# A graph-network kernel: gated sums of two destination tiles accumulated in PSUM and added once, with half-tile weight buffers

## The chip, the cores and the metric

The kernel runs on one core of a Trainium2 chip. The time is that of the device, in microseconds (us), from the first to the last instruction with what the launch adds around them. The median of three runs counts.

## The reference

Four layers of a graph network over 6250 nodes with 128 features and 206250 edges, sorted by destination. Each layer normalises the rows, applies a relu, sums rows over edges, and adds to `x`. Only the first layer weights its edges, and it is the one that the change touches.

```python
h = jnp.maximum(_layernorm(x, axis=-1), 0.0)
g = sigmoid(h @ W_gate + b_gate)
m = g * (h @ W)
msgs = edge_weight[:, None] * m[dst]
x = x + segment_sum(msgs, src, num_segments=6250)   # first layer
x = x + segment_sum(h[src], dst) @ W1.T + b1        # second; third and fourth alike
```

## The kernel before

**Tiles and stages.** Nodes are cut into 49 tiles of 128 (`TILES`). Five stages follow one another: a preparation (to about 130 us in the profile), the *count stage* (to about 1328 us), and three and a bit more stages (`ph` 1 to 4) that multiply by count matrices read back from DRAM (`by_source`). The change lies in the preparation and the count stage.

**One step of the count stage** (`build(j, k, c)` on each engine) handles destination tile `j`, with 128 edge slots in 64 windows. DVE makes one-hot operands out of the edge records in eight groups of eight windows (`hots`: L882, L883, L885), in `HOT_SLOTS` = 3 buffers. PE multiplies them (`half_windows`, L602 to L604: 12 matmuls of 98 columns in each of 16 *units*), which gives the plain counts and the weighted counts of this destination against all 49 source tiles, in one of three pairs of PSUM banks. ACT copies plain counts and the high half of the weighted ones to `stage` (L1174, `hi_done`); PE subtracts the high half in PSUM (`take_high`, L585), and ACT copies the rest, the low half (L1159, `lo_done`). PE cannot be more than two units ahead of those copies: before unit `u` it subtracts the high half of unit `u-2`, which waits for its `hi_done`.

**The SP queue** (`hand_on`) then hands the tile on, in order: a small load `g_in`, a DMA that transposes the high weights (49 blocks of 128x128) into `wt`, the same two for the low weights, and a store of the plain counts to DRAM. `stage` and `wt` each have two buffers, by the parity of the tile. ACT waits at the first unit of tile `j` until the store of tile `j-2` has landed (`stored0`, `stored1`), and SP waits for `hi_done` of the whole tile.

**The gated sums.** `sum_four(t, b, g)` multiplies four blocks of `wt` of tile `t` with its gated rows `g_in`: 12 matmuls of 128 columns into one of two PSUM banks (L577 to L579), 147 in a tile. DVE adds each bank to `X` (`add_four`, L897), 13 times in a tile. PE does this for tile `j-2` while it builds tile `j`, two such fours behind each group of windows.

**The loop.** `tiles_loop` writes out 13 tiles and then loops three times over 12. All engines have the same shape. The edge records (`meta`, `meta_w`) of all 25 pairs of tiles stay in SBUF; the preparation fills them in five batches.

Of the kernel before, what the change touches and what calls it, by code (L numbers as in the profile page):

```python
# [19 lines left out]
P = 128  # L20
# [38 lines left out]
FULL = TILES + TILES % 2  # L59
SET_COLS = HALF * WD  # L60
# [27 lines left out]
def summed_at(h):  # L88

    return range(2 * h, min(2 * h + 2, FOURS))  # L90
# [64 lines left out]
def gnn_kernel(nc, x, src, dst, edge_weight, w0, wg0, bg0, w1, b1, wm, bm, wu, bu, hyper, w3, b3, gamma, beta, out):  # L155
    ctx = ExitStack()
    with ctx:
# [21 lines left out]
        table = nc.dram_tensor("edge_table", (ROWS, 3 * ALIGN), I32).ap()  # L179
        by_source = nc.dram_tensor("counts_by_source", (FULL // 2, P, TILES, 2, P), F16).ap()  # L180
# [16 lines left out]
        mv = keep("mv", [P, TILES, 2], F32)  # L197
# [13 lines left out]
        meta, o = at("meta", [P, GROUPS, 2, P // 2, 2], F16, base0)  # L211
        meta_w, o = at("meta_w", [P, WINDOWS // 2, WEIGHTS, 2], F16, o)
# [28 lines left out]
        G, o = at("G", [P, TILES, 2, P], F16, wt_at)  # L241
        pre, r = at("pre", [P, BATCH, 2, P], F16, o)
# [95 lines left out]
        def _(sp):  # L338
# [18 lines left out]

            def turn_keys(m):

                lot = batch(m)  # L360
                sp.wait_ge(s("pre"), m + 1)
                sp.dma_start_transpose(meta[:, lot.start:lot.stop].rearrange("e n a q b -> e (n a) (q b)"),
                                       pre[:].rearrange("q n a e -> q (n a e)")).then_inc(s("keys_in"), 16)
                if m:
                    sp.wait_ge(s("meta_w"), m)
# [9 lines left out]
            for m in range(3):  # L375
                turn_keys(m)
            store_gated(0)
# [4 lines left out]
            for c in range(3, SET):  # L382
                store_gated(c)

            def layers(general):
                if general:
                    for a, b in ((dst, dst_pad), (src, src_pad), (edge_weight.bitcast(I32), w_pad)):
                        sp.dma_start(b[0:EDGES].rearrange("(a b) -> a b", a=15), a.rearrange("(a b) -> a b", a=15)).then_inc(s("pad_in"), 16)
# [8 lines left out]
                sp.wait_ge(s("g_stored"), 16 * SET)  # L397

                def hand_on(j, k, c):

                    b = c % 2
                    if later(j, 2):
                        sp.wait_ge(s("four_done"), (j - 1) * FOURS)
                    for a, done in enumerate(("hi_done", "lo_done")):
                        part = slice(a * P, (a + 1) * P)
                        sp.wait_ge(s(done), (j + 1) * HALVES)
                        sp.dma_start(g_in[:, b, part], slab(g_dram, j)[:, part]).then_inc(s(f"g_loaded{b}"), 16)
# [289 lines left out]
        def _(dve):  # L697
# [172 lines left out]
            def layers(general):  # L870
# [59 lines left out]
                def split(ph):  # L930

                    if ph == 1:
                        counts_stored(dve)
# [360 lines left out]
```

## Time and profile before

| what | value |
|---|---|
| median of three runs | 2605.35 us (2597.77 to 2607.53) |
| the profiled execution | 2608.04 us |
| its span | 2606.2 us |
| busy PE / DVE / ACT | 2320.7 / 1603.8 / 1230.0 us |
| DVE adds of L897 | 637, 392.4 us busy |
| matmuls of L577 to L579 | 3 x 2401 |
| stores of counts, transposes into `wt` | 49 and 98 DMAs |

Busy time is what an engine spent inside instructions. A busy PE is not a PE at its peak, since its matmuls overlap. The granted clock is the share of full speed that TensorE got: 1.00 is 2.4 GHz and 0.50 is 1.2 GHz.

### The profile page before, as it was taken

The numbers are of one execution on the slowest core, as the hardware profiler recorded it, in microseconds if no ns is written. First come the engines' busy times: TensorE is split into PE (matmuls) and PEld (weight loads), VectorE is DVE, ScalarE is ACT, GpSimd is POOL, SyncE is SP. The second block draws the span as 40 slices with busy tenths as digits, with TensorE's granted clock in tenths as the row PEclk, the third lists the DMA queues.
The fourth block names the chain that finished last, engine by engine and source line by source line (L and its number), as shares of the span: only waits on it lengthen the run. The fifth ranks groups of instructions, "written<-read, shape, count | busy, mean of one in ns | idle before, by whom it ended". The sixth has DMA issues, their size and how long they took to land. (4 is left out here: it accounts for less than half of the span.)

```text
span 2606.2 us, 71305 instructions
## 1 busy us (share of the span) xinstructions
PE 2320.7 (89%) x27901; PEld 1993.0 (76%) x27901; DVE 1603.8 (62%) x3678; ACT 1230.0 (47%) x2680; POOL 44.6 (2%) x51
## 2 busy tenths in 40 slices
PE   2489999999989998999929999899998999999996
PEld 1368778878777887887828888788887888888884
DVE  6689999999999998999962333334433112121224
ACT  2478878878777786877731222222232000011113
POOL 3300000000000000000000000000000000000000
PEclk8589999999999998999969999999998999999996
DMA  6479999999999999999989999899998999999994
GB/s 191 106 157 201 216 214 208 210 218 209 212 181 220 212 212 175 222 199 212 218 211 251 283 285 283 223 260 258 258 259 208 290 288 290 263 246 248 266 270 110
DMA packets 1608879, 589.27 MB, mean 226 GB/s; under 512 B 964326, under 2 KB 1605354, under 8 KB 1608471
## 3 DMA queue, kind: packets, MB, share of 16 engines
q1 hardware_dynamic: 1604773, 579.88, 99.9%
q0 software_dynamic: 1600, 4.92, 0.7%
q8 instruction: 191, 3.13, 0.5%
q10 hardware_dynamic: 2226, 0.62, 0.2%
q14 instruction: 89, 0.73, 0.1%
HBM read 255.26 MB, written 89.20 MB: 132 GB/s over the span
## 5 line engine op out<-in xcount | busy, mean ns | idle before, releaser
L1174 ACT CAST stage<-ps 128x784 f16<-128x784 f32 x784 | 655.4, 836 | 106.0 <-DMA counts_by_source<-stage 69.7
L649 PE MATMUL ps<-Ha,a_tiles 128*128 128x258 f16 x4802 | 548.5, 274 | 46.6 <-ACT Ha L1221 39.2
L649 PEld LDWEIGHTS ps<-Ha,a_tiles 128*128 128x128 f16 x4802 | 470.1, 98 | 117.1 <-ACT Ha L1221 39.3
L602 PE MATMUL ps<-hot_c,hot_r 128*128 128x98 f16 x3136 | 509.5, 212 | 13.6 <-DVE hot_c L885 7.4
L603 PE MATMUL ps<-hot_c,hot_r 128*128 128x98 f16 x3136 | 503.5, 211 | 0.0
L604 PE MATMUL ps<-hot_c,hot_r 128*128 128x98 f16 x3136 | 501.7, 210 | 0.0
L1159 ACT CAST stage<-ps 128x392 f16<-128x392 f32 x784 | 397.9, 508 | 142.5 <-PE ps L585 142.5
L577 PE MATMUL ps<-g_in,wt 128*128 128x128 f16 x2401 | 431.0, 222 | 35.9 <-DVE X L897 17.3
L578 PE MATMUL ps<-g_in,wt 128*128 128x128 f16 x2401 | 429.3, 222 | 0.0
L579 PE MATMUL ps<-g_in,wt 128*128 128x128 f16 x2401 | 429.2, 222 | 0.0
L897 DVE SCALAR_TENSOR_TENSOR X<-ps,X 128x512 f32<-128x512 f32 (+1 forms) x637 | 392.4, 650 | 49.4 <-PE ps L579 49.3
L602 PEld LDWEIGHTS ps<-hot_c,hot_r 128*128 128x128 f16 x3136 | 308.7, 98 | 95.8 <-ACT stage L1159 53.0
L885 DVE TENSOR_TENSOR hot_c<-hot_c,meta_w 128x1568 f16<-128x1568 f16 x392 | 378.6, 966 | 0.0
L603 PEld LDWEIGHTS ps<-hot_c,hot_r 128*128 128x128 f16 x3136 | 310.5, 99 | 19.2 <-issue 1.9
L585 PE MATMUL ps<-stage,minus 128*128 128x392 f16 x784 | 262.9, 335 | 59.2 <-ACT stage L1174 30.8
L604 PEld LDWEIGHTS ps<-hot_c,hot_r 128*128 128x128 f16 x3136 | 309.9, 99 | 0.0
L649 PE MATMUL ps<-Hb,a_turned 128*128 128x258 f16 x2401 | 277.9, 274 | 14.3 <-DMA a_turned<-counts_by_source 12.0
L649 PE MATMUL ps<-Hb,a_tiles 128*128 128x258 f16 x2401 | 278.4, 274 | 7.2 <-ACT Hb L1200 7.2
L577 PEld LDWEIGHTS ps<-g_in,wt 128*128 128x128 f16 x2401 | 238.0, 99 | 59.7 <-DVE X L897 42.9
L649 PEld LDWEIGHTS ps<-Hb,a_turned 128*128 128x128 f16 x2401 | 233.4, 98 | 52.0 <-DMA a_turned<-counts_by_source 15.2
L649 PEld LDWEIGHTS ps<-Hb,a_tiles 128*128 128x128 f16 x2401 | 235.1, 98 | 48.1 <-ACT Hb L1200 7.4
L883 DVE TENSOR_TENSOR hot_r<-iota_r,meta 128x1024 f16<-128x1024 f16 x392 | 267.5, 682 | 0.0
(194 smaller groups left out, 2062.1 us busy)
## 6 DMA issues: line engine op xcount, KB each, us to landing
a_tiles<-counts_by_source SPq DMA_DIRECT2D x147, 1600.0 KB, 8.8
counts_by_source<-stage SPq DMA_DIRECT2D x49, 1600.0 KB, 8.0
gated_parts<-G SPq DMA_DIRECT2D x7, 448.0 KB, 3.6
g_in<-gated_parts SPq DMA_DIRECT2D x98, 32.0 KB, 3.1
out_x<-X SPq DMA_DIRECT2D x6, 512.0 KB
edge_table<-tab SPq DMA_DIRECT2D x1, 2448.0 KB, 10.5
wt<-stage SPq DMA_TRANSPOSE x98, 10.9
dst_run<-in_dst SPq DMA_DIRECT2D x1, 612.4 KB
```

Of the source, the lines that this page charges most:

```text
L577: mm(o, wt[:, b, 0, i], g_in[:, b, 0:P], start=i % 4 == 0, stop=False, skip_group_check=True)
L578: mm(o, wt[:, b, 0, i], g_in[:, b, P:2 * P], start=False, stop=False, skip_group_check=True)
L579: last = mm(o, wt[:, b, 1, i], g_in[:, b, 0:P], start=False, stop=True, skip_group_check=True)
L602: mm(into(0), rows_, codes(0), start=v == 0, stop=True, skip_group_check=True)
L603: mm(into(1), rows_, codes(1), start=v == 0, stop=False, skip_group_check=True)
L604: last = mm(into(1), rows_, codes(2), start=False, stop=True, skip_group_check=True)
L649: last = mm(ps[:, c % 2, 0:PARTS], a_slot(ph, c, i), moving[:, i], start=i == 0, stop=i == TILES - 1)
L883: v.tensor_tensor(hot_r[:, b], iota_r[:].unsqueeze(1).to_broadcast([P, PAIRS, P, 2]), key(0, P), ALU.is_equal)
L885: v.tensor_tensor(hot_c[:, b, :, 1:1 + WEIGHTS], hot_c[:, b, :, 0].unsqueeze(2).to_broadcast([P, PAIRS, WEIGHTS, WCOLS, 2]), meta_w[:, pai ...
L897: v.scalar_tensor_tensor(xs, ps[:, 6 + e, 0:(hi - lo) * P], 1.0 / (W_UP * H_UP), xs, ALU.mult, ALU.add).then_inc(s("added"), 1)
L1159: a.copy(stage[:, b, 2, 0:TILES, u * SET_COLS:(u + 1) * SET_COLS], of).then_inc(s("lo_done"), 1)
L1174: a.copy(stage[:, b, 0:2, 0:TILES, u * SET_COLS:(u + 1) * SET_COLS], of).then_inc(s("hi_done"), 1)
```

## The change

1. **Sums of two tiles in PSUM.** `sum_four` now works on a pair of tiles: for each of four source tiles it accumulates the three products of the first tile and the three of the second in the same bank, 24 matmuls, and `add_four` adds the bank once. The fours of a pair are spread over two steps: six (`FIRST`) in the odd tile behind groups 1 to 6, seven in the even tile after it, behind groups 0 to 6. They come one tile later than before: pair `n` (tiles `2n`, `2n+1`) is summed in tiles `2n+3` and `2n+4`.
2. **Half-tile weight buffers.** A tile's weights are held in two halves (24 and 25 blocks), in six homes that rotate (`HOMES`), so each transposing DMA becomes two. `stage` keeps its two buffers, one block each shorter.
3. **Edge records streamed.** The preparation turns the records into `keys_b` and `weights_b`, stores them by pair of tiles to DRAM (`edge_groups`), and SP loads the record of pair `p+2` (128 KB) when the one-hot operands of pair `p` are done. The interleaving copy on POOL becomes two copies.

```diff
+def fours_at(c, h):
+    if c % 2:
+        return range(h - 1, h) if 1 <= h <= FIRST else range(0)
+    return range(FIRST + h, FIRST + h + 1) if FIRST + h < FOURS else range(0)
...
-        stage, o = at("stage", [P, 2, 1 + WEIGHTS, FULL, P], F16, o)
+        stage, o = at("stage", [P, 2, PARTED, P], F16, o)
-        wt, o = at("wt", [P, 2, WEIGHTS, TILES, P], F16, o)
-        g_in, o = at("g_in", [P, 2, 2 * P], F16, o)
+        wt, o = at("wt", [P, 6, WEIGHTS, len(HALF_TILES[1]), P], F16, o)
+        g_in, o = at("g_in", [P, 4, 2 * P], F16, o)
...
+            def store_groups(m):
+                lot = batch(m)
+                sp.wait_ge(s("meta_w"), m + 1)
+                sp.wait_ge(s("keys_in"), 16 * (m + 1))
+                to = groups[lot.start:lot.stop].rearrange("n e x -> e n x")
+                sp.dma_start(to[:, :, 0:KEYS], keys_b[:, m % 2]).then_inc(s("meta_stored"), 16)
+                sp.dma_start(to[:, :, KEYS:], weights_b[:, m % 2]).then_inc(s("meta_stored"), 16)
...
                 def hand_on(j, k, c):
-                    b = c % 2
-                    if later(j, 2):
-                        sp.wait_ge(s("four_done"), (j - 1) * FOURS)
+                    b, pair = c % 2, pair_of(k, c)
+                    if b:
+                        sp.wait_ge(s("hot_ready"), j * TILE_HOTS + TILE_HOTS)
+                        sp.dma_start(meta[:, to], of).then_inc(s(f"meta_in{to}"), 16)
+                    if b and later(j, 2):
+                        sp.wait_ge(s("four_done"), (pair - 1) * FOURS + FIRST)
+                    elif later(j, 4):
+                        sp.wait_ge(s("four_done"), (pair - 1) * FOURS)
                     for a, done in enumerate(("hi_done", "lo_done")):
                         sp.wait_ge(s(done), (j + 1) * HALVES)
-                        sp.dma_start_transpose(wt[:, b, a], stage[:, b, 1 + a, 0:TILES].rearrange("p i d -> p (i d)")).then_inc(s(f"wt_in{b}"), 16)
+                        for half, tiles in enumerate(HALF_TILES):
+                            first = FULL + a * TILES + tiles.start
+                            sp.dma_start_transpose(wt[:, home(c, half), a, 0:len(tiles)],
+                                                   stage[:, b, first:first + len(tiles)].rearrange("p i d -> p (i d)")).then_inc(s(f"wt_in{b}"), 16)
...
-                def sum_four(t, b, g):
+                def sum_four(n, cp, g, both=True):
-                    n, e = t * FOURS + g, (b + g) % 2
+                    f, e = n * FOURS + g, (cp + g) % 2
                     for i in range(4 * g, min(4 * g + 4, TILES)):
                         o = ps[:, 6 + e, (i % 4) * P:(i % 4 + 1) * P]
-                        mm(o, wt[:, b, 0, i], g_in[:, b, 0:P], start=i % 4 == 0, stop=False, skip_group_check=True)
-                        mm(o, wt[:, b, 0, i], g_in[:, b, P:2 * P], start=False, stop=False, skip_group_check=True)
-                        last = mm(o, wt[:, b, 1, i], g_in[:, b, 0:P], start=False, stop=True, skip_group_check=True)
+                        for b in range(1 + both):
+                            at_ = wt[:, home(c, half), :, i - HALF_TILES[half].start]
+                            mm(o, at_[:, 0], g_in[:, c % 4, 0:P], start=i % 4 == 0 and b == 0, stop=False, skip_group_check=True)
+                            mm(o, at_[:, 0], g_in[:, c % 4, P:2 * P], start=False, stop=False, skip_group_check=True)
+                            last = mm(o, at_[:, 1], g_in[:, c % 4, 0:P], start=False, stop=True, skip_group_check=True)
                     last.then_inc(s("four_done"), 1)
```

**On DVE**, the rows from the last groups of an odd tile written out ahead of the loop to the first group of the next tile. Before, two adds stand behind a group, one short add at the end of a tile's fours, and one group has none (`meta` and `meta_w` hold the records):

```order
L897 SCALAR_TENSOR_TENSOR X<-ps,X 128x512 [waits added,four_done] x2
L882 TENSOR_TENSOR hot_c<-iota_c,meta 128x4x196 [waits unit_done]
L883 TENSOR_TENSOR hot_r<-iota_r,meta 128x1024
L885 TENSOR_TENSOR hot_c<-hot_c,meta_w 128x4x392 [waits hot_codes]
L897 SCALAR_TENSOR_TENSOR X<-ps,X 128x128 [waits added,four_done]
L882 TENSOR_TENSOR hot_c<-iota_c,meta 128x4x196 [waits unit_done]
L883 TENSOR_TENSOR hot_r<-iota_r,meta 128x1024
L885 TENSOR_TENSOR hot_c<-hot_c,meta_w 128x4x392 [waits hot_codes]
```

In the changed kernel, over the same kind of boundary (`meta` holds keys and weights of a pair):

```order
L962 SCALAR_TENSOR_TENSOR X<-ps,X 128x512 [waits added,four_done]
L947 TENSOR_TENSOR hot_c<-iota_c,meta 128x4x196 [waits meta_in0,unit_done]
L948 TENSOR_TENSOR hot_r<-iota_r,meta 128x1024
L950 TENSOR_TENSOR hot_c<-hot_c,meta 128x4x392 [waits hot_codes]
L962 SCALAR_TENSOR_TENSOR X<-ps,X 128x512 [waits added,four_done]
L947 TENSOR_TENSOR hot_c<-iota_c,meta 128x4x196 [waits unit_done]
L948 TENSOR_TENSOR hot_r<-iota_r,meta 128x1024
L950 TENSOR_TENSOR hot_c<-hot_c,meta 128x4x392 [waits hot_codes]
```

At most one add now stands behind a group, and the first group of a pair waits for its record.

**On the SP queue**, one tile in the loop before (an ISA row is a wait or an address):

```order
L406 ISA [waits four_done]
L407 ISA [waits hi_done]
L407 DMA g_in<-gated_parts 128x128
L408 DMA_TRANSPOSE wt<-stage 128x49x128
L407 ISA [waits lo_done]
L407 DMA g_in<-gated_parts 128x128
L408 DMA_TRANSPOSE wt<-stage 128x49x128
L409 ISA
L409 DMA counts_by_source<-stage 128x25x256
```

and one odd tile of the changed kernel:

```order
L446 ISA [waits hot_ready]
L446 DMA meta<-edge_groups 128x512
L449 ISA
L454 ISA [waits four_done]
L455 ISA [waits hi_done]
L455 DMA g_in<-gated_parts 128x128
L458 DMA_TRANSPOSE wt<-stage 128x24x128
L458 DMA_TRANSPOSE wt<-stage 128x25x128
L455 ISA [waits lo_done]
L455 DMA g_in<-gated_parts 128x128
L458 DMA_TRANSPOSE wt<-stage 128x24x128
L458 DMA_TRANSPOSE wt<-stage 128x25x128
```

The store of the counts (L460) follows as before. Two more DMAs stand between a tile's last copy and its store, and an odd tile's record load stands ahead of them.

## Rows read from the trace of the kernel before

**Rows 1.** Windows, 300:600: busy time by engine, clock, DMA share, GB/s

```profile
300.00:600.00 300.00, 281.32 (x4553) 242.12 (x4551) 297.47 (x477) 240.31 (x411) 0.00 (x0) 0.99 1.08 213
```

**Rows 2.** Timeline of DVE near 740: start us, us, line, what, how many

```profile
738.33 0.55 DVE L882 TENSOR_TENSOR hot_c<-iota_c,meta 128x784 f16<-128x784 f16 x1
...
740.29 1.28 DVE L897 SCALAR_TENSOR_TENSOR X<-ps,X 128x512 f32<-128x512 f32 x2
741.49 0.55 DVE L882 TENSOR_TENSOR hot_c<-iota_c,meta 128x784 f16<-128x784 f16 x1
...
746.81 0.55 DVE L882 TENSOR_TENSOR hot_c<-iota_c,meta 128x784 f16<-128x784 f16 x1
...
748.78 0.56 DVE L882 TENSOR_TENSOR hot_c<-iota_c,meta 128x784 f16<-128x784 f16 x1
```

**Rows 3.** Timeline of PE near 401, same columns

```profile
400.55 0.33 PE L585 MATMUL ps<-stage,minus 128*128 128x392 f16 x1
...
401.28 0.33 PE L585 MATMUL ps<-stage,minus 128*128 128x392 f16 x1
...
402.03 0.22 PE L577 MATMUL ps<-g_in,wt 128*128 128x128 f16 x1
...
403.37 0.33 PE L585 MATMUL ps<-stage,minus 128*128 128x392 f16 x1
```

**Rows 4.** Timeline of the SP queue from 434: start, length of each issue

```profile
434.45 7.97 SPq L408 DMA_TRANSPOSE wt<-stage  x1
442.46 0.58 SPq L407 DMA_DIRECT2D g_in<-gated_parts  x1
443.09 7.98 SPq L408 DMA_TRANSPOSE wt<-stage  x1
451.12 0.58 SPq L409 DMA_DIRECT2D counts_by_source<-stage  x1
457.28 0.36 SPq L407 DMA_DIRECT2D g_in<-gated_parts  x1
```

**Rows 5.** Timeline of ACT around two tiles' starts, idle time before in brackets

```profile
433.13 0.88 ACT L1174 CAST stage<-ps 128x784 f16<-128x784 f32 x1
...
435.95 0.81 ACT L1174 CAST stage<-ps 128x784 f16<-128x784 f32 x1 [1.55 <-DMA counts_by_source<-stage]
...
437.04 0.83 ACT L1174 CAST stage<-ps 128x784 f16<-128x784 f32 x1
...
456.21 0.88 ACT L1174 CAST stage<-ps 128x784 f16<-128x784 f32 x1
...
459.08 0.81 ACT L1174 CAST stage<-ps 128x784 f16<-128x784 f32 x1 [1.60 <-DMA counts_by_source<-stage]
```

**Rows 6.** Waits, 300 to 600 us: total us, times, longest

```profile
ACT stage L1174 <- DMA counts_by_source<-stage: 21.5, 12, 3.2
```

**Rows 7.** Timeline of PE at 624, idle time before in brackets

```profile
623.96 0.51 PE L585 MATMUL ps<-stage,minus 128*128 128x392 f16 x1 [2.19 <-ACT stage L1174]
```

**Rows 8.** Windows of 1 us just behind it, columns as Rows 1

```profile
624.00:625.00 1.00, 1.00 (x10) 0.72 (x11) 1.00 (x3) 1.00 (x3) 0.00 (x0) 0.50 1.27 245
...
627.00:628.00 1.00, 1.00 (x18) 1.00 (x16) 0.07 (x1) 0.67 (x1) 0.00 (x0) 0.83 1.26 213
```

**Rows 9.** Windows of 2 us, stage 4, over a boundary of two transposes

```profile
2446.00:2448.00 2.00, 2.00 (x21) 1.74 (x19) 0.00 (x0) 0.00 (x0) 0.00 (x0) 1.00 1.27 289
2448.00:2450.00 2.00, 1.76 (x17) 1.43 (x15) 0.36 (x2) 0.77 (x4) 0.00 (x0) 1.00 0.83 154
```

**Rows 10.** Timeline of the SP queue: stores of tiles 0 and 24

```profile
168.55 0.58 SPq L409 DMA_DIRECT2D counts_by_source<-stage  x1
...
733.67 0.45 SPq L409 DMA_DIRECT2D counts_by_source<-stage  x1
```

**Rows 11.** Timeline of ACT at the start of tile 2

```profile
177.10 0.81 ACT L1174 CAST stage<-ps 128x784 f16<-128x784 f32 x1 [6.49 <-DMA counts_by_source<-stage]
```

**Rows 12.** Waits, 1290 to 1400 us

```profile
PE ps L577 <- DMA wt<-stage: 8.6, 1, 8.6
```

**Rows 13.** Timeline of the SP queue before the count stage

```profile
121.20 1.35 SPq L362 DMA_TRANSPOSE meta<-pre  x1
122.60 1.54 SPq L366 DMA_TRANSPOSE turned_w<-pre_w  x1
```

**Rows 14.** Timeline of POOL before the count stage

```profile
126.27 1.26 POOL L483 COPY meta_w<-turned_w 128x1280 f16<-128x1280 f16 x1 [11.69 <-DMA turned_w<-pre_w]
```

More of the change, by code:

```diff
@@ L376, in _ @@
                 turn_keys(m)
+            sp.wait_ge(s("meta_stored"), 32)
+            for n in range(2):
+                sp.dma_start(meta[:, n], groups[n]).then_inc(s(f"meta_in{n}"), 16)
             store_gated(0)
@@ L381, in _ @@
             turn_keys(4)
-            for c in range(3, SET):
+            for c in range(3, SET - 1):
                 store_gated(c)
+            store_groups(BATCHES - 1)
+            spare = (BATCHES - 1) % 2
+            sp.dma_start(groups[GROUPS, :, 0:KEYS], keys_b[:, spare, 0]).then_inc(s("meta_stored"), 16)
+            sp.dma_start(groups[GROUPS, :, KEYS:], weights_b[:, spare, 0]).then_inc(s("meta_stored"), 16)
+            store_gated(SET - 1)
             def layers(general):
                 if general:
+                    for n in range(2):
+                        sp.wait_ge(s(f"meta_in{n}"), 16)
                     for a, b in ((dst, dst_pad), (src, src_pad), (edge_weight.bitcast(I32), w_pad)):
@@ L480, in interleave @@
                 pool.wait_ge(s("weights_turned"), 16 * (m + 1))
-                lot = batch(m)
-                pairs = meta_w[:, lot.start * P // 2:lot.stop * P // 2].rearrange("p q a b -> p a q b")
-                g.tensor_copy(pairs, turned_w[:].rearrange("p a (q b) -> p a q b", b=2)).then_inc(s("meta_w"), 1)
+                if m >= 2:
+                    pool.wait_ge(s("meta_stored"), 32 * (m - 1))
+                to = weights_b[:, m % 2].rearrange("p n (q a b) -> p a n q b", q=P // 2, b=2)
+                for a in range(WEIGHTS):
+                    last = g.tensor_copy(to[:, a], turned_w[:, a].rearrange("p (n q b) -> p n q b", n=BATCH, b=2))
+                last.then_inc(s("meta_w"), 1)
             def high_parts(c):
@@ L619, in build @@
                         half_windows(j, c % 2, c, 2 * h + 1)
-                        if later(j, 2):
-                            sums(j - 2, c % 2, k * (SLOTS // 2) + c // 2, h)
+                        for g in fours_at(c, h):
+                            if not isinstance(n, int) or n >= 0:
+                                if g == 0:
+                                    loaded(n, 0)
+                                    loaded(n, 1)
+                                sum_four(n, cp, g)
                 if general:
@@ L1169, in build @@
                             act.wait_ge(s(f"stored{b}"), n * 16)
[L1170 removed]
+                            act.wait_ge(s(f"wt_in{b}"), n * 64)
                         act.wait_ge(s("unit_done"), j * HALVES + (u + 1))
```

118 lines of the change are left out of this document (67 added, 51 removed).

## The prediction

> **What bounds the kernel now.** I read the busy times of stretches first, to see which stage the change touches and which engine is full there. In the count stage DVE is busy 297.47 of 300 us, PE 281.32, ACT 240.31, and the DMA engines are as good as full (share 1.08) [rows 1]. So DVE looks like the bound. The timelines say how near the others are.
>
> DVE: from one group's first instruction to the next one's is 3.16 us with two adds and 1.97 us without [rows 2]. An add thus costs 0.595 us. A tile is 8 x 1.97 + 12 x 0.595 + 0.2 for the short add = 23.1 us.
>
> PE: a unit takes 0.73 to 0.75 us, and 24 sum matmuls take 1.34 us, 0.056 each [rows 3]. A tile is 16 x 0.74 + 147 x 0.056 = 20.1 us. ACT: a high and a low copy take 1.09 us [rows 5], so a tile is 17.4 us.
>
> Then the chain through the DMA queue, which no busy share shows. Call h the end of a tile's last high copy, and S the moment at which its `stage` buffer is free for the tile after next. Tile 12 ends at 433.13 + 0.88 = 434.01 [rows 5]. SP issues two transposes of 8.0 us one after the other, and the store at 451.12, 17.1 us after h [rows 4]. It lands 8.0 us later, at S = 459.08, where ACT has been waiting [rows 5]. S - h is C = 25.1 us. From S of one tile to its h is X: 435.95 to 457.09, 21.1 us [rows 5]. Two tiles per turn of this loop take C + X = 46.2 us, 23.1 a tile: **the loop through the stage buffers is as tight as DVE.** ACT waited there in 12 of some 13 tiles, 21.5 us in all [rows 6]. The mean from store to store is (733.67 - 168.55) / 24 = 23.55 us [rows 10], 0.45 above DVE's own pace: DMA and the clock cause that part.
>
> **The change part by part.**
>
> *Adds.* A pair of tiles needs 13 adds for 26. DVE per tile falls to 15.76 + 3.85 = 19.6 us. If DVE alone were the bound, PE would bound at 20.1 and a tile would gain 3.4 us. But C does not contain DVE. What can shrink is X.
>
> *X without DVE's limit.* At S, PE stands before unit 2 of the tile. By hand, from the durations above: ACT's first copy 0.8; PE's units 2 and 3, 1.5, with 0.6 of waiting for ACT's second copy and the low copy; one four, 1.3. That is 4.2 us to the end of group 1. In an odd tile of the new kernel five groups with a four follow (5 x 2.82 = 14.1), then one of 1.5 without, then ACT's last copies, 1.3: **X = 21.1 us in an odd tile.** An even tile has done one four ahead of the stall and its last is short: four groups of 2.82, one of 1.8, one of 1.5 and the rest give 20.1. The same matmuls are there as before (24 x 13 less the missing blocks is 2 x 147 per pair). They were spread two behind a group, the first two ahead of the stall; in an odd tile now none is ahead of it. What DVE gives back is partly taken by that.
>
> *C.* The halved transposes issue the same blocks: an issue of 10 blocks takes 1.35 to 1.54 us [rows 13], one of 49 takes 8.0 [rows 4], about in proportion, so no fixed part shows. The record load is issued ahead of h, while SP is idle (from 451.7 to 457.3 here [rows 4]). If that cover is gone it costs 0.6 us of issue per pair. The bubble between two transposes is a cost on the DMA side: a window with such a boundary moved 154 GB/s for 289 [rows 9], 0.9 us lost per boundary. While SP's issue is what paces a transpose, the bubble is caught up. From below the two new boundaries cost nothing, from above 1.9 us a tile. I take C = 25.0: an even tile between shortens the backlog that an odd one meets.
>
> *The clock.* An even tile lasts about 20.4 us, so the odd one after it meets its buffer 25.0 - 20.4 = 4.6 us late. PE has only units 0 and 1 to do meanwhile, and stands still for about 5 us. In the trace 2.19 us without work [rows 7] left the granted clock at 0.50 from 624 until during 627 [rows 8]; that is 1.2 GHz for 3.4 us, in which PE loses 1.7 us of work. Some of it falls in the 0.6 us of waiting, so X of an odd tile grows by about 1.0. Then 2 tiles take 25.0 + 21.1 + 1.0 = 47.1 us: **23.55 us a tile, what it is now.** With the clock kept it is 46.1, or 23.05.
>
> The Trainium skill ("TensorE: Matmul & The Clock Gate", section "HAM oscillation — how this bites in real kernels") says that a wait for DMA in every turn of a loop can throttle the array in every turn. By that rule a tile takes 23.55, without it 23.05. The trace agrees with it for a single wait [rows 7, 8].
>
> *SP, waits added.* An odd tile's SP waits for `hot_ready` before the record load. Behind it stands the hand-on of that tile, which needs its last high copy anyway, later than its last one-hot. DVE's wait for `meta_in` is on a load issued two tiles earlier. PE's wait for the second tile's weights comes in group 1 two tiles on, more than 20 us after the 17.1 us of issue and a landing. None costs time.
>
> *Start.* Tile 2 has no sums now. It starts at 177.10 when its buffer comes [rows 11], and then goes at ACT's 17.4 instead of DVE's 23.1: -5 us, taking a little off for PE.
>
> *End.* Behind the last build stand pair 23 (294 matmuls, 16.5 us) and tile 48 (147). Before, tile 47's 147 were followed by 8.6 us of waiting for tile 48's weights [rows 12]. The extra work fills most of this wait, and tile 48's sums start when they did, with less idle time before them; a clock fall of up to 1.7 us is saved: -2 us.
>
> *Preparation.* In the last batch SP issues two stores ahead of the weight transpose (122.60 [rows 13]), each between 0.6 [rows 4] and 1.5 us [rows 13], and POOL's copy of 1.26 us [rows 14] becomes two, +0 to 1.3. DVE's last G tiles wait behind that copy. 1.2 to 4.3 us, I take +2.5, the middle.
>
> **The sum:** -5 - 2 + 2.5 + 46 x (23.55 - 23.55) = -4.5 us against the profiled execution's 2608.04, whose span is 2606.2. The median is 2605.35, so 2601; I say 2600.
>
> **The rivals.**
>
> *Forecast: the stage loop takes over from DVE.* For it: ACT's wait in nearly each tile, and C that holds SP issue and landing only. Against: X is built by hand. Chance 0.42, 2585 to 2618.
>
> *Faster: the loop is shorter than I make it.* The wait spreads evenly over odd and even tiles so that the clock stays up, X is 20.5 and C is 24.5 because the DMA queue is less often behind. A tile takes 22.5, 46 x -1.05 = -48 us and the -4.5: 2553. For it: DVE is full now and would have 4 us to catch up with after each disturbance. Against: the odd tile has no four before the stall. It decides as soon as C + X of odd tiles falls below 46.7, which with the -4.5 makes 0.5%. Even PE's 20.1 a tile is excluded by C: it would need X = 15. Chance 0.32.
>
> *Slower: the DMA queue becomes the bound.* The two extra transposes and half a record load per tile bring 2.5 boundaries of 0.9 us. For it: a share of 1.08 [rows 1], and a mean of 23.55 where DVE alone makes 23.1. Against: SP's issue paces the transposes, and SP has 5.5 us of idle time in a tile. If half is not caught up, C grows by 1.7 at full clock falls: 24.4 a tile, +39 - 4.5: 2640. If nothing is, 2680. It decides from 0.75 us more in C + X. Chance 0.26.
>
> The Trainium skill ("DMA: Bandwidth & Descriptors", section "Anatomy of one DMA — SWDGE (gpsimd) path") gives a DMA about 2 us of fixed cost, mostly completion, which speaks against splitting. By it C would grow by up to 4 us and a tile would take 25.5, near 2690. The issues show no such part [rows 4, 13], and DMAs follow one another there without waiting for completion, so it has a small part, 0.05, of the slower case.
>
> **The numbers.** A change of 0.5%, 13 us, is what a measurement of this kernel can tell from none. Faster: the faster rival and a fifth of the forecast, 0.32 + 0.08 = 0.40. Slower: the slower rival and a little of the forecast, 0.28. Same: 0.32. The range, 2535 to 2650, takes in the faster rival's time and the half-paid bubbles, leaving 0.1 on either side. The forecast's own is 2585 to 2618.
>
> **What would show it.** DVE's busy share in the stage falls to about 0.83. ACT's wait for the store grows to above 3 us in odd tiles and goes towards nothing in even ones, and the clock shows a dip in most odd tiles. Store to store stays near 23.5 on average, with long and short ones in turn. Tile 2 ends 5 us earlier. The prediction is wrong if the periods fall below 23 (the loop was not the bound), if PE waits for `wt` DMAs, or if C rises above 26 (the bubbles are paid).

## The result, and the profile after

The changed kernel takes 2651.14 us (median of 4 runs, 2648.51 to 2653.32). The kernel before, run beside it, takes 2606.44. The ratio is 1.0168, with an interval from 1.015 to 1.0187: **slower by 1.7%, 44.7 us**. The forecast was 2600 with a range up to 2650, so the time lies 1 us above the range and near the price of the slower rival (2640). The profiled execution has a span of 2646.4 us against 2606.2.

The window that answers to [rows 1]: span, then busy PE, PEld, DVE, ACT, POOL, granted clock, DMA share, GB/s.

```profile
300.00:600.00 300.00, 268.21 (x4306) 236.25 (x4307) 239.55 (x367) 231.79 (x391) 0.00 (x0) 0.94 1.08 206
```

DVE went from 99% busy to 80%, as the adds were halved. But PE did less work too in these 300 us (4306 matmuls, 4553 before) and moved at a clock of 0.94. The one column that did not get lighter is DMA: the same share of 1.08, though with fewer tiles done in the time it moved 206 GB/s for 213. No compute engine is full now.

Two groups of instructions on the page's fifth part: busy time, mean ns of one, then the idle time just before them and what ended it.

```profile
L1238 ACT CAST stage<-ps 128x784 f16<-128x784 f32 x784 | 653.8, 834 | 156.5 <-DMA counts_by_source<-stage 114.9
L962 DVE SCALAR_TENSOR_TENSOR X<-ps,X 128x512 f32<-128x512 f32 (+1 forms) x325 | 214.2, 660 | 231.3 <-PE ps L637 229.3
```

The adds are 325 for 637, and take 214.2 us for 392.4: 178.2 us of DVE's work are gone. In their place DVE waits 231.3 us, for PE. ACT's first copy of a tile waits 114.9 us for a store of counts to land (69.7 in the kernel before).

The waits from 300 to 600 us (total us, times, longest) answer to [rows 6]:

```profile
DVE X L962 <- PE ps L637: 53.8, 68, 8.2
ACT stage L1238 <- DMA counts_by_source<-stage: 34.4, 11, 5.5
PE ps L643 <- ACT stage L1238: 32.0, 12, 5.7
```

Read from the bottom: PE waits 32.0 us for ACT, ACT waits 34.4 us for the store (21.5 before), and DVE waits for both. It is one chain, and it starts at the DMA.

**Two tiles of it.** ACT's timeline at the ends of tiles 11 (odd), 12 and 13 and the starts of 13 and 14, which answers to [rows 5]:

```profile
420.68 0.83 ACT L1238 CAST stage<-ps 128x784 f16<-128x784 f32 x1
421.76 0.86 ACT L1238 CAST stage<-ps 128x784 f16<-128x784 f32 x1
...
442.15 0.89 ACT L1238 CAST stage<-ps 128x784 f16<-128x784 f32 x1
447.93 0.81 ACT L1238 CAST stage<-ps 128x784 f16<-128x784 f32 x1 [4.50 <-DMA counts_by_source<-stage]
...
469.26 0.83 ACT L1238 CAST stage<-ps 128x784 f16<-128x784 f32 x1
471.66 0.81 ACT L1238 CAST stage<-ps 128x784 f16<-128x784 f32 x1 [1.18 <-DMA counts_by_source<-stage]
```

Tile 11 ends at 420.68 + 0.83 = 421.51, and tile 12 starts at once, at 421.76: its buffer is free. It ends at 442.15 + 0.89 = 443.04: 21.5 us. Tile 13 may start only at 447.93, when tile 11's store has landed, 26.4 us after tile 11's end, and ends at 470.09: 27.05 us. This is the C of the prediction (from a tile's end, h, to its buffer free, S), 26.4 where it had 25.0.

The SP queue over the same time (start, length of each issue; x2 is a pair of halves), against [rows 4]:

```profile
421.96 8.10 SPq L458 DMA_TRANSPOSE wt<-stage  x2
430.10 0.58 SPq L455 DMA_DIRECT2D g_in<-gated_parts  x1
430.73 8.02 SPq L458 DMA_TRANSPOSE wt<-stage  x2
438.79 0.93 SPq L460 DMA_DIRECT2D counts_by_source<-stage  x1
443.11 0.94 SPq L455 DMA_DIRECT2D g_in<-gated_parts  x1
444.10 9.63 SPq L458 DMA_TRANSPOSE wt<-stage  x2
453.77 0.58 SPq L455 DMA_DIRECT2D g_in<-gated_parts  x1
454.40 8.36 SPq L458 DMA_TRANSPOSE wt<-stage  x2
462.81 0.59 SPq L460 DMA_DIRECT2D counts_by_source<-stage  x1
```

The even tile's first pair takes 9.63 us, for 7.97 of one whole transpose before. It begins 5.3 us after a store of 1600 KB was issued, which is still on its way.

What the wait of 4.50 us does to PE: its first instruction behind it, and then windows of 1 us (columns as in [rows 1]).

```profile
448.79 0.51 PE L643 MATMUL ps<-stage,minus 128*128 128x392 f16 x1 [4.58 <-ACT stage L1238]
```

```profile
449.00:450.00 1.00, 1.00 (x12) 0.82 (x12) 0.00 (x0) 1.00 (x3) 0.00 (x0) 0.50 1.25 276
450.00:451.00 1.00, 1.00 (x13) 0.85 (x11) 0.00 (x0) 0.85 (x2) 0.00 (x0) 0.50 0.69 118
451.00:452.00 1.00, 1.00 (x14) 1.00 (x13) 0.00 (x0) 0.89 (x3) 0.00 (x0) 0.50 1.86 33
452.00:453.00 1.00, 1.00 (x19) 1.00 (x18) 0.00 (x0) 0.50 (x1) 0.00 (x0) 0.92 0.59 127
```

After 4.58 us of idling PE's clock is at 0.50 for some 3.4 us, and then full again.

**The whole count stage.** I measured h, S, C and X of every tile in both traces. T is the time from one h to the next, and X the time from S to the tile's h; the rows by parity are means over tiles 5 to 48 without the two in which the loop turns (25 and 37). S counts as the start of the tile's first high copy.

| us | before, odd / even | after, odd / even |
|---|---|---|
| T | 23.45 / 23.45 | 27.20 / 21.97 |
| X, where S was waited for | 21.25 / 21.28 | 22.35 / 20.63 |
| C, where S was waited for | 25.4 / 25.5 | 26.7 / 28.4 |
| h to the store's issue | 17.0 / 17.3 | 18.1 / 19.5 |
| S after the h of the tile just before, all tiles | 1.92 / 1.89 | 4.85 / 0.96 |
| mean T, tiles 5 to 48, all | 23.87 | 24.81 |

C and X of an odd tile, 26.7 + 22.35 = 49.05 us, are the time of a pair, for 47.1 forecast. In the kernel before they made 25.45 + 21.25 = 46.7, so the pair got 2.35 us longer: 1.25 of it are C and 1.1 are X. The span's +40.2 us then falls on: the preparation +2.6 (end of tile 0 at 155.08 for 152.52), tiles 1 to 4 -0.4, tiles 5 to 48 44 x 0.934 = +41.1, and all behind -3.1. Nearly all is in the pace of the loop. (The profiled executions are 40.5 us apart, 2648.51 against 2608.04, the medians 44.7.)

One thing was already in the trace of before: most of its tiles take 23.06 to 23.10 us, DVE's pace, and seven of the 42 take 24.4 to 25.8, in which C is 26.3 to 26.9. The two bounds were nearly equal, and the tiles whose C was long went at the pace of the DMA chain.

### The profile page after: what moved, and what is told of

It reads as the page before. It is cut to its first block and busy times, and to the rows that moved or that the text cites. A ratio compares the mean times of both kernels' runs of the same rounds, so it can differ in the third digit from the quotient of the medians.

```text
span 2646.4 us, 69590 instructions
## 1 busy us (share of the span) xinstructions
PE 2323.7 (88%) x27901; PEld 2011.0 (76%) x27901; DVE 1445.9 (55%) x3366; ACT 1236.5 (47%) x2680; POOL 44.7 (2%) x56
## 5 line engine op out<-in xcount | busy, mean ns | idle before, releaser
L1238 ACT CAST stage<-ps 128x784 f16<-128x784 f32 x784 | 653.8, 834 | 156.5 <-DMA counts_by_source<-stage 114.9
L660 PE MATMUL ps<-hot_c,hot_r 128*128 128x98 f16 x3136 | 523.3, 215 | 17.3 <-DVE hot_c L950 9.8
L661 PE MATMUL ps<-hot_c,hot_r 128*128 128x98 f16 x3136 | 517.6, 214 | 0.0
L662 PE MATMUL ps<-hot_c,hot_r 128*128 128x98 f16 x3136 | 515.7, 214 | 0.0
L660 PEld LDWEIGHTS ps<-hot_c,hot_r 128*128 128x128 f16 x3136 | 314.0, 100 | 105.0 <-ACT stage L1223 60.3
L643 PE MATMUL ps<-stage,minus 128*128 128x392 f16 x784 | 269.6, 344 | 130.6 <-ACT stage L1238 113.8
L950 DVE TENSOR_TENSOR hot_c<-hot_c,meta 128x1568 f16<-128x1568 f16 x392 | 379.2, 967 | 2.0 <-issue 2.0
L962 DVE SCALAR_TENSOR_TENSOR X<-ps,X 128x512 f32<-128x512 f32 (+1 forms) x325 | 214.2, 660 | 231.3 <-PE ps L637 229.3
L661 PEld LDWEIGHTS ps<-hot_c,hot_r 128*128 128x128 f16 x3136 | 316.7, 101 | 21.3 <-issue 1.0
L662 PEld LDWEIGHTS ps<-hot_c,hot_r 128*128 128x128 f16 x3136 | 316.7, 101 | 0.0
## 6 DMA issues: line engine op xcount, KB each, us to landing
edge_table<-tab SPq DMA_DIRECT2D x1, 2448.0 KB, 10.5
```

The source lines that it names most:

```text
L643: mm(o, minus16[:], stage[:, b, FULL:FULL + TILES, u * SET_COLS:(u + 1) * SET_COLS], start=False, stop=True, skip_group_check=True).then_i ...
L660: mm(into(0), rows_, codes(0), start=v == 0, stop=True, skip_group_check=True)
L661: mm(into(1), rows_, codes(1), start=v == 0, stop=False, skip_group_check=True)
L662: last = mm(into(1), rows_, codes(2), start=False, stop=True, skip_group_check=True)
L950: v.tensor_tensor(hot_c[:, b, :, 1:1 + WEIGHTS], hot_c[:, b, :, 0].unsqueeze(2).to_broadcast([P, PAIRS, WEIGHTS, WCOLS, 2]), weights[:, at ...
L1238: a.copy(stage[:, b, 0:2 * FULL].rearrange("p (k i) d -> p k i d", k=2)[:, :, 0:TILES, u * SET_COLS:(u + 1) * SET_COLS], of).then_inc(s("h ...
```

## The experiments

Three theories stood after this. **A**: halving the transposes makes the DMA part of the loop longer. **B**: the unequal tiles do it (an even tile at PE's pace, then a wait with nothing for PE to do, then half a clock). **C**: the record loads disturb the queue. Each kernel was compared with the kernel before on the same chip; its median there is 2593.18, 2606.48, 2592.59 or 2607.88 us, so ratios are compared and not times. The one trace of the kernel before comes from a chip with 2606.44. On those with 2593 the first copy of the count stage starts 12 to 14 us earlier in the variants of the kernel before (120.3 to 122.3 for 134.6), which is about the whole difference, so T is compared across chips too. A trace shows one execution; three lie more than 5 us from their kernel's median: before_halved 6.2 above, before_store_one_gated 5.8 above, before_act_store 6.5 below.

**1. before_halved: one part of the change alone.** The kernel before with each transpose cut in two.

```diff
-sp.dma_start_transpose(wt[:, b, a], stage[:, b, 1 + a, 0:TILES]...)
+for lo, hi in ((0, 24), (24, TILES)):
+    sp.dma_start_transpose(wt[:, b, a, lo:hi], stage[:, b, 1 + a, lo:hi]...)
```

> The kernel before with each transposing DMA issued as two (24 and 25 blocks) into the same buffer, nothing else. Theory A (the halves cost DMA time, which lengthens the chain from a tile's end to its free stage buffer): the chain rises from 25.5 to 26.5 us or more, a tile takes 23.9 to 24.4 us instead of 23.45, +20 to +40 us. Theory B (the odd and even wave of the fours makes the loss, the halves are caught up): no change, within 8 us of before.

Measured: 2617.37 against 2593.18, ratio 1.0081 (1.0048 to 1.0113). T is 24.56 for 23.87, and C 26.5 to 27.1 for 25.5. How long SP took to issue a transpose from 300 to 600 us (min/median/max ns), in this kernel:

```profile
L409 SPq DMA_TRANSPOSE wt<-stage x50: 3591/4200/5824, 296.6 to 598.4; - x50
```

and in the kernel before:

```profile
L408 SPq DMA_TRANSPOSE wt<-stage x27: 7349/7828/8667, 293.6 to 596.7; - x27
```

Two halves take 8.4 us for one whole of 7.8; from h to the store it is 18.3 us for 17.1. So halving alone costs 0.69 us a tile and 30 us by the trace. But the traced execution, 2623.59, is the slowest of four. By the medians the cost is 24 us, by the ratio 21. This is theory A, and about half of the loss: 0.8% (0.5 to 1.1) of the changed kernel's 1.7%. What is left is for the parts below.

**2. before_short_adds: DVE relieved alone, in odd tiles.** The adds of odd tiles keep 8 of their 512 columns, so most of the gated sums of odd tiles are left out.

```diff
-v.scalar_tensor_tensor(xs, ps[:, 6 + e, 0:(hi - lo) * P], ...)
+n_ = 8 if b else (hi - lo) * P
+v.scalar_tensor_tensor(xs[:, 0:n_], ps[:, 6 + e, 0:n_], ...)
```

> The kernel before, in which DVE adds only 8 of 512 columns of each four in odd tiles, so half of the add time leaves DVE and all waits stay. It leaves out most of the gated sums of odd tiles. If the stage loop bounds as tightly as DVE: DVE's share falls to about 0.85 and a tile still takes 22.8 to 23.3 us, -10 to -30 us. If DVE alone were the bound: PE's 20.1 us a tile, -100 us or more.

Measured: 2603.94 against 2593.18, ratio 1.0023 (0.9998 to 1.0048), T 24.14. Its waits from 300 to 600 us:

```profile
DVE X L898 <- PE ps L579: 46.7, 43, 6.1
ACT stage L1175 <- DMA counts_by_source<-stage: 30.7, 8, 5.9
```

The waits of the changed kernel appear here with whole transposes and no other change: ACT's wait for the store grows from 21.5 to 30.7 us. DVE, 97% busy from 300 to 1200 us, lost 12 points of load (762 for 869 us in 900), and the kernel gained nothing, where 10 to 30 us were expected. Only odd tiles were relieved, so this run brings an unevenness of its own (T 23.14 in odd and 24.62 in even tiles); a relief of all tiles alike, without other changes, was not run.

**3. after_no_records: the loads of records left out.** The loop uses the first records again and again, so the edges are wrong.

```diff
-sp.wait_ge(s("hot_ready"), j * TILE_HOTS + TILE_HOTS)
...
-sp.dma_start(meta[:, to], of).then_inc(s(f"meta_in{to}"), 16)
```

> The changed kernel without the record loads in the loop: all pairs use the records of the first two, so the sums are those of wrong edges; every other instruction stays. Theory A: the load is 1 of 6 DMAs per pair and its boundary counts about half a us per tile in the odd tile's chain: -10 to -25 us against the changed kernel. Theory B (wave): no change, within 8 us.

Measured: ratio 1.0155 (1.0124 to 1.0186), T 24.83 with the loads gone and 24.81 with them. The two ratios differ by 0.1%, within their intervals, where 10 to 25 us were expected if the loads cost anything. Theory C is out.

**4. after_four_first: a four for PE ahead of the wait.** In odd tiles the six fours stand behind groups 0 to 5 and not 1 to 6.

```diff
-return range(h - 1, h) if 1 <= h <= FIRST else range(0)
+return range(h, h + 1) if h < FIRST else range(0)
```

> The changed kernel with an odd tile's six fours behind groups 0 to 5 instead of 1 to 6: PE has 1.3 us of sums to do while it waits for the buffer, and 1.3 us less afterwards. Theory of the loop (two tiles take chain plus X of the odd tile): X of odd tiles falls from 22.35 to about 21.0 us, two tiles take 47.7 instead of 49.05, -25 to -32 us against the changed kernel. Rival (the DMA queue itself is full and sets 49 us for two tiles): the chain grows by what X loses, no change.

Measured: 2628.94 against 2593.18, ratio 1.0135 (1.0104 to 1.0166), for 1.0168 of the changed kernel. T is 24.58: odd tiles 25.85, even ones 22.86. PE's wait fell from 32.0 to 21.3 us in 300, X of odd tiles from 22.35 to 21.49. But C of odd tiles grew from 26.7 to 27.2. PE's wait, from 300 to 600 us:

```profile
PE ps L643 <- ACT stage L1238: 21.3, 12, 4.4
```

So this edit is worth about 0.2 us a tile, 10 us by the trace and 9 by the ratios (whose intervals overlap a little), a third of what I expected: half of what X gives back, C takes. It is not the price of theory B as a whole, for two thirds of PE's wait and most of the unevenness are still there.

**5 and 6. The store ahead of the transposes.** If S is what everyone waits for, SP can issue the store first. ACT then waits for the store and the high transpose at its first unit, and for the low one at unit 2. Done in both kernels.

```diff
+sp.wait_ge(s("hi_done"), (j + 1) * HALVES)
+sp.dma_start(two_tiles(j), ...).then_inc(s(f"stored{b}"), 16)
 for a, done in enumerate(("hi_done", "lo_done")):
     ...
-sp.dma_start(two_tiles(j), ...).then_inc(s(f"stored{b}"), 16)
```

> The kernel before with the store of the counts issued ahead of the transposes, and ACT waiting for the store and the high weights at unit 0 and for the low weights only at unit 2 of the tile after next. Same DMAs, same bytes. If the chain through the queue is what bounds: the buffer's first part is free some 15 us after a tile's end, its last part after 21 us, so the loop no longer binds and DVE does with 23.1 us a tile: -10 to -25 us, and the dips of the clock go. If the DMA queue's capacity bounds instead: unchanged, within 8 us.

> The changed kernel with the same new order of the queue. If the chain bounds: it falls to PE's pace (21.5 us as its even tiles have it) or to the DMA queue's capacity, 22.5 us a tile for 24.8: -80 to -140 us against the changed kernel, faster than both. If the queue's capacity is what makes 49 us for two tiles: unchanged.

Measured: before_store_first 2609.18 against 2606.48, ratio 1.0011 (1.0 to 1.0022): no gain, though ACT's wait for the store is gone. PE waits for transposes instead, 17.1 us from 300 to 1200 us, and why T stays at 23.80 and does not reach DVE's 23.1 is open. after_store_first 2619.15, ratio 1.0054 (1.0036 to 1.0071), some 30 us less than the changed kernel, T 23.98. That lies between the two expectations, 80 to 140 us and nothing. ACT now waits for transposes (57.4 us in 25 waits from 300 to 1200 us), and SP's queue has hardly a gap left:

```profile
451.70 8.34 SPq L460 DMA_TRANSPOSE wt<-stage  x2
460.47 0.35 SPq L446 DMA_DIRECT2D meta<-edge_groups  x1
461.09 0.42 SPq L449 DMA_DIRECT2D counts_by_source<-stage  x1
461.86 3.55 SPq L457 DMA_DIRECT2D g_in<-gated_parts  x1
465.46 10.28 SPq L460 DMA_TRANSPOSE wt<-stage  x2
475.93 0.44 SPq L457 DMA_DIRECT2D g_in<-gated_parts  x1
476.41 8.12 SPq L460 DMA_TRANSPOSE wt<-stage  x2
```

A `g_in` load of 32 KB is held up for 3.55 us behind the store, and the pair after it takes 10.28. From 450 to 1150 us SP spends 95% of the time inside DMA issues, and its gaps above 0.4 us add up to less than 1%. The share is 79% in the changed kernel, 70% in the one before and 90% in before_store_first. So in the changed kernel SP's queue was not full: the length of the chain, with the store last in it, is what bound, and the order alone gives back 1.1 of the 1.7%, with the same DMAs. With the chain shortened, the full queue sets the pace: about 24.0 us a tile with halves.

**7. after_store_four_first: both of these edits.**

```diff
-return range(h - 1, h) if 1 <= h <= FIRST else range(0)
+return range(h, h + 1) if h < FIRST else range(0)
```

(on top of the store first)

> As after_store_first, and an odd tile's fours one group earlier. If the wait for the buffer is gone, no more than 10 us further; if some of it is left, the gain of the four shows as it did alone, about 10 us.

Measured: 2635.48 against 2606.48, ratio 1.011 (1.0093 to 1.0128), T 24.41. Worse than the store first alone, where up to 10 us less were expected. The waits from 300 to 600 us show what is late now:

```profile
PE ps L636 <- DMA wt<-stage: 21.7, 6, 4.7
```

The first four needs the weights of the tile before last, and they come later when the store goes first. A four ahead of the wait is of use only when its own weights are there.

**8. before_quartered: is it the number of DMAs?** The kernel before with each transpose cut in four.

```diff
+for lo, hi in ((0, 12), (12, 24), (24, 36), (36, TILES)):
+    sp.dma_start_transpose(wt[:, b, a, lo:hi], stage[:, b, 1 + a, lo:hi]...)
```

> The kernel before with each transposing DMA issued as four (12, 12, 12 and 13 blocks). Two halves made the issue of a tile's weights 1.3 us longer, 0.65 us per added DMA. If each added DMA costs that: six of them make SP's part 3.9 us longer than before, a tile about 2 us longer than before, +80 to +90 us. If splitting costs once: as the halves, +25 us.

Measured: 2643.52 against 2606.48, ratio 1.0144 (1.0125 to 1.0163): 37 us, where a cost by the piece made 80 to 90. T is 24.65 (24.56 with halves), C 27.4, h to store 18.4 to 18.8. By the traces, from the first copy of tile 0 to the end of the last tile, quarters cost 33.5 us and halves 30.3, but the halves' trace is that of their slowest execution, 6 us above the median. A piece takes 2.07 us on average, four of them 8.3: no more than two halves (8.4 to 8.5). So in SP's issue only the first cut shows. In the time it costs 21 to 24 us (two more DMAs a tile), and cutting in four instead of two, with four more, another 13 to 16: less by the piece, but not nothing.

**9 and 10. The store's data taken out of the queue.** The store keeps 128 of its 1600 KB, and 49 full stores follow after the stage, so all tiles get the counts of the last two. The totals (2825 and 2764 us, one execution each) mean nothing; the pace within the stage does.

```diff
-sp.dma_start(two_tiles(j), stage[:, b, 0]...)
+sp.dma_start(two_tiles(j)[:, 0:2], stage[:, b, 0, 0:4]...)
```

> The kernel before with each tile's store cut from 25 to 2 pieces (1600 to 128 KB), and 49 full stores issued behind the count stage, so only the pace of tiles counts here, not the total. All tiles get the counts of the last two. If the DMA queue's capacity makes 23.45 us a tile: the pace falls to DVE's 23.1 us, with ACT never waiting for a store.

> The changed kernel with the same cut, wrong counts likewise, and the total likewise without meaning. If the queue is what eats the saved adds: tiles go at PE's pace, 20.5 to 21.5 us, where the changed kernel has 24.8, and the saved adds are worth 1.6 to 2.6 us a tile against the kernel before with the same cut. If the wave of the fours or PE itself makes the loss: odd and even tiles stay at some 27 and 21.5 us.

Windows, 300 to 600 us, of before_small_store and then of after_small_store:

```profile
300.00:600.00 300.00, 282.75 (x4616) 244.12 (x4614) 300.00 (x482) 245.12 (x417) 0.00 (x0) 1.00 0.88 150
```

```profile
300.00:600.00 300.00, 296.23 (x4950) 259.98 (x4948) 277.47 (x426) 262.62 (x447) 0.00 (x0) 1.00 0.97 163
```

With room in the queue the kernel before runs at DVE's pace, 23.09 us a tile, DVE busy all the time. The changed one runs at 21.53 in odd and even tiles alike, PE busy 296 of 300 us at full clock. **This is the gain that the change gives when DMA is out of the way: 1.56 us a tile, 67 us from the end of tile 0 to the end of tile 48. In the real kernels the path through the DMA queue takes it all, and 0.9 us a tile more.** The small store both empties the queue and ends the chain sooner (it lands some 21 us after h, for 26.7 to 28.4), so these two runs do not tell capacity from latency; experiments 5 and 6 do. They also show the waves and the clock dips to be a consequence: they are gone with the wait, though the fours stand where they stood.

**11 and 12. The store on ACT's own DMA queue**, issued at the second unit of the next tile, in both kernels.

```diff
+def store_counts(j, b):
+    act.wait_ge(s("hi_done"), (j + 1) * HALVES)
+    act.dma_start(two_tiles(j), ...).then_inc(s(f"stored{b}"), 16)
...
+if u == 1 and later(j, 1):
+    store_counts(j - 1, 1 - b)
```

> The kernel before with the store of the counts issued on ACT's DMA queue at unit 1 of the next tile instead of behind the transposes on SP's. If the two queues' transfers overlap and fill each other's bubbles: the wait for the store goes, DVE's 23.1 us bounds, -10 to -20 us. If they only share the same DMA engines: ACT's waits move to the weights, within 8 us of before. If ACT's issue is held up by a full queue: slower by 10 to 50 us.

> The changed kernel with the store on ACT's queue likewise. Overlap: the pace falls below 24 us to 22 or 23, faster than both kernels, -60 to -100 us against the changed one. No overlap: as with the store issued first, 24.0 us a tile, -30 us. ACT held up: no gain.

Measured: before_act_store 2599.24 against 2592.59, ratio 1.0034 (1.0014 to 1.0053), T 23.73: as expected if the queues only share what they have. after_act_store 2644.13, ratio 1.02 (1.0171 to 1.0228), T 24.87. The SP queue of before_act_store:

```profile
429.30 10.14 SPq L408 DMA_TRANSPOSE wt<-stage  x1
441.13 0.36 SPq L407 DMA_DIRECT2D g_in<-gated_parts  x1
441.53 10.49 SPq L408 DMA_TRANSPOSE wt<-stage  x1
```

A transpose takes 10.1 to 10.5 us to issue, for 8.0 in [rows 4]. The store overlaps them now, the two of a tile take 4 to 5 us longer together, and the store itself lands 14 us after its issue, for 8: the second queue adds no capacity here. In the changed kernel 30 us less were expected even so, as in after_store_first, and there is no gain at all: ACT's wait has moved to the slower transposes. In after_act_store, from 300 to 600 us:

```profile
ACT stage L1243 <- DMA wt<-stage: 31.8, 11, 4.6
```

**13 and 14. One small DMA fewer.** With the store first, the two `g_in` loads of 32 KB became one of 64 KB, in both kernels. If each DMA costs the queue something, this gives back a part of what the two extra ones cost.

```diff
-for a, done in enumerate(("hi_done", "lo_done")):
-    part = slice(a * P, (a + 1) * P)
...
-    sp.dma_start(g_in[:, b, part], slab(g_dram, j)[:, part])
...
+        if a:
...
+            sp.dma_start(g_in[:, b], slab(g_dram, j))
```

> before_store_first with the two 32 KB loads of gated rows per tile joined into one of 64 KB between the transposes: same bytes, one DMA less in the queue. If the number of DMAs is what costs capacity (0.65 us for each one added): the queue needs 22.7 us and DVE's 23.1 us a tile bounds, -10 to -20 us against before. If only the bytes count: as before_store_first, within 5 us of before.

> after_store_first with the same joining. If the number of DMAs costs: 23.98 us a tile falls to 23.2 to 23.5, -20 to -35 us against after_store_first, at or below the time of before. If only the bytes count: no change against after_store_first.

Measured: 2614.12 against 2607.88, ratio 1.0022 (1.0007 to 1.0037), and 2631.53, ratio 1.0075 (1.0049 to 1.01). T is 24.01 and 24.32, for 23.80 and 23.98 with two loads. The queue of after_store_one_gated:

```profile
443.40 0.53 SPq L453 DMA_DIRECT2D counts_by_source<-stage  x1
443.98 13.48 SPq L460 DMA_TRANSPOSE wt<-stage  x2
```

The 3.55 us that the small load stood behind the store are now in the pair behind it (13.48 for 10.28). Over the stage the first pair of a tile takes 14.0 us for 9.4, as much more as the load had taken (4.2). Nothing comes back: taking a small load out of this queue gains nothing, and a cut in a transpose costs.

No version beat both kernels.

## Why the prediction was wrong, point by point

**The step that failed is the one on C: "so no fixed part shows", "While SP's issue is what paces a transpose, the bubble is caught up", "I take C = 25.0".** C of odd tiles is 26.7, above the 26 that the prediction itself named as a sign of being wrong. Of the +1.7, 0.4 is that I took C from one tile, and its mean was 25.45 already. The other 1.3 are 1.1 of issue (h to store 18.1 us for 17.0) and 0.2 of landing. The argument "about in proportion" compared a transpose of 10 blocks, issued in the preparation, with one of 49 in the stage. That can't show what a cut costs in the stage. Experiment 1 measured it, with nothing else changed: C +1.0 to +1.6, T +0.69 (0.55 by the medians).

**The second half of that step, "an even tile between shortens the backlog", didn't show.** Pairs of halves in odd tiles take 8.4 us on average, as in experiment 1. The even tile starts its hand-on when the odd tile's store is still moving, and its first pair takes 9.0 us on average (9.6 in the rows above). Its C is 28.4, but this is off the path: the odd tile after it goes by the odd tile's own C.

**The sum hid a second step.** It set a bare C + X of 47.1 us a pair against 23.55 us a tile, a measured mean that holds the disturbed tiles of the kernel before. By the prediction's own rows the bare sum of before was 46.2. The forecast thus had the loop 0.9 us a pair longer, some 21 us in all, and put it at nothing, without a reason why the new loop should be free of the disturbances. Bare sums compared, it is 49.05 for 46.7.

**X was right to about half a us.** Forecast 21.1 + 1.0 for the clock in an odd tile, measured 22.35; forecast 20.1 in an even one, measured 20.63. The even tile lasts 21.97 for a forecast of 20.4: at best it lasts 21.53, which is also the pace of PE in experiment 10. My 20.1 for PE's work in a tile was 1.4 too low. The sum for two tiles was 25.0 + 22.1 = 47.1, and is 26.7 + 22.35 = 49.05: 1.7 of the 1.95 are C. X's growth of 1.1 over the kernel before was forecast, and it is a part of the loss all the same.

**The wave and the clock came out as forecast, the wave by luck.** Odd tiles meet their buffer 4.85 us late (4.6), but that is 26.7 less an even tile of 21.97, where I had 25.0 less 20.4: two errors of 1.6 to 1.7 us that cancel. In the rows above PE stands 4.6 us (5) and the clock is at 0.50 for 3.4 us (3.4), and ACT's wait is above 3 us in all odd tiles and 0 to 2.4 in even ones. The stretch at 0.50 is 3.4 us in nine of the 20 odd tiles without a turn, and 6.8 in eleven, more than I had. The mean clock of the stage fell from 0.98 to 0.94. The Trainium skill ("TensorE: Matmul & The Clock Gate", section "HAM oscillation — how this bites in real kernels") says that a wait for DMA that recurs in a loop throttles the array anew each time; the trace agrees, with a stretch at 0.50 at the wait of each odd tile from 5 on. What that costs was not separated. In experiment 10, at full clock and without a wait, X of odd tiles is 21.3 us for 22.35, and in experiment 4 more work for PE ahead of the wait gave 10 us. The miss against the forecast is not here, since the 1.0 for the clock was in it.

**DVE's relief** was as computed (a share of 0.80 for a forecast of 0.83) and is worth nothing here, as the stage loop said; experiment 2 shows the same for odd tiles relieved alone.

**The small terms.** Preparation: +2.5 forecast, +2.6 measured. SP's two stores and the later weight transpose stand where they were expected, against [rows 13], and POOL's copy starts 2.5 us later (128.80 for 126.27):

```profile
121.45 1.35 SPq L391 DMA_TRANSPOSE keys_b<-pre  x1
122.90 0.63 SPq L383 DMA_DIRECT2D edge_groups<-keys_b  x1
123.58 0.55 SPq L384 DMA_DIRECT2D edge_groups<-weights_b  x1
124.18 2.00 SPq L395 DMA_TRANSPOSE turned_w<-pre_w  x1
```

End: -2 forecast, -3.1 measured. PE's wait for the last weights (8.6 in [rows 12]) is now

```profile
PE ps L635 <- DMA wt<-stage: 2.8, 1, 2.8
```

Start: -5 forecast, -0.4 measured. Tile 2 did end early (25.4 us for 29.5), but tile 3 met its buffer only 30.1 us after tile 1's end. In the kernel before too the store of tile 1 landed 28.9 us after that tile's end; there tile 2 was still at work. The forecast left out this buffer of the next tile. SP does issue the first record load just ahead of tile 1's hand-on, into a queue with a store in it:

```profile
171.96 0.58 SPq L460 DMA_DIRECT2D counts_by_source<-stage  x1
172.59 5.36 SPq L446 DMA_DIRECT2D meta<-edge_groups  x1
```

That took 5.36 us where I had allowed 0.6 "if that cover is gone". But without it (experiment 3) the `g_in` load behind the store takes 5.29 us, and tile 3 starts 30.0 us after tile 1's end: the record load is not the reason.

**The rival that came true** is the slower one, "the DMA queue becomes the bound". Its price, C + 1.7, 24.4 a tile and 2640, hit C by luck: half of its 2.5 boundaries of 0.9 us makes only 1.1, and 0.4 of the measured +1.7 stood in the kernel before. The time came out 11 us longer. Against the profiled execution of before it is 5.7: the start +4.6, the pace +2.0, the preparation +0.1, the end -1.1. The rest is that the medians lie further apart than the profiled executions. Its reason, a loss at each boundary, is not confirmed: 2.5 boundaries more come with 1.3 us in C, but six more for whole transposes cut in four cost 37 us and not three times the 21 to 24 of two, and removing a small load gives nothing.

The Trainium skill ("DMA: Bandwidth & Descriptors", section "Anatomy of one DMA — SWDGE (gpsimd) path") gives about 2 us of fixed cost a DMA, for DMAs that GpSimd issues; the ones here are issued by SP. It warned in the right direction. The measurement decides on the size: two extra DMAs in C cost 1.0 to 1.6 us together and not 4, and two more cuts of each transpose another 0.3 to 0.9 us.

**What stays open.** Why the first cut of each transpose costs 0.5 to 0.7 us a tile while taking out a small DMA of the same queue gives nothing. A pair of halves takes 0.5 to 0.7 us more to issue than one whole, and nothing in the traces says for what. The other half of the loss, X of odd tiles with its missing four and its clock, is argued from the table and experiments 2, 4 and 10; no run has it alone. A changed kernel with whole transposes was not tried: its rotating half-tile homes need two DMAs, and whether homes for whole tiles fit in SBUF is open.

## What to carry to other kernels

An engine that is 99% busy is not worth relieving when a second loop is nearly as long: here DVE's 23.09 us a tile stood beside a chain through the DMA queue that made it 23.45, and taking 45% off the adds gave nothing. Compare bare sums with bare sums, and measured means with measured means. Before valuing a relief, add up the chain through each double buffer, from the end of a tile's work to the buffer free and on to the end of the next, and take the largest transfer out of the queue for one run, as in experiments 9 and 10, which tells what the relief is worth without it. When transposes are on that chain, don't pay for a buffer scheme by cutting them, and take the price of a cut from the loop it will stand in. The order of a queue is worth a run too: the store ahead of the transposes gave back 1.1 of the 1.7%.

## What the runs showed of the hardware that was not expected

- A transpose of 49 blocks takes SP 7.8 us to issue, two of 24 and 25 take 8.4 to 8.5, four of 12 or 13 take 8.3. In the issue the step is between one and two; in the kernel's time four cost 1.4% and two 0.8%.
- A 1600 KB store on another engine's queue slows the transposes beside it (10.1 to 10.5 us each for 8.0), and the kernel gains nothing (ratios 1.0034 and 1.02, for 1 and 1.0168).
- A load of 32 KB issued right behind that store holds SP for 3.9 to 4.2 us on average (0.3 to 0.7 in the ordinary order); without it the next transposes take as much longer. So the length of an issue tells of what was issued ahead of it, and not of the DMA alone.
- From 300 to 1200 us all variants with the full store move 200 to 209 GB/s, whatever their order. Since each tile moves the same bytes, that is the pace of the tiles told in another unit, and shows no ceiling by itself.
